# A second mixture of experts that sends each row to its two experts, in place of one that runs all eight

## The chip, the cores and the metric

One core of a Trainium2 chip runs the whole program. The metric is the device time of one execution in microseconds (us), median over runs. The engines are TensorE (PE, with its weight loads PEld), VectorE (DVE), ScalarE (ACT), GpSimd (POOL) and SyncE (SP), which issues DMAs.

## The reference

The program is two rounds of graph attention and mixture of experts over 6250 nodes of 256 features. Only its last step is touched:

```python
tokens = layernorm(x)                                   # 6250 x 256
probs = softmax(tokens @ router_w.T)                    # 8 experts
rw, re = top_k(probs, 2); rw = rw / max(rw.sum(-1), 1e-12)
out = tokens
for e in range(8):
    h = gelu(tokens @ w1[e] + b1[e])                    # 256 -> 256
    y = h @ w2[e] + b2[e]                               # 256 -> 256
    out = out + combine[:, e:e+1] * y                   # combine is 0 but for the two best
x = x + out
```

Everything is float32. The nodes are padded to 6400, which is 50 blocks of 128 rows.

## The kernel before

The program is a row of phases with a barrier (`end_phase`) between them. All node rows stay in one buffer in SBUF, `node`, of 51 blocks of 264 columns. Names in the trace carry the phase: `attn_` attention over edges, `gate_` the first mixture's router, `exp_` its experts, `pr_` projections for the second graph layer, `rel_` that layer, and `moe_` the second mixture, the last phase and the one that is replaced.

`feed_forward_top2` takes one block a turn. DVE divides the sums of the graph layer by their denominators (L2337 to L2340), adds the saved `x2` (L2342), takes the statistics (L587, L590), normalizes (L659) and adds the normalized row to `node` (L2325). PE transposes (L669), computes the router's logits (L2265), then for all eight experts the hidden features (`hidden`, L2227, four groups of four column tiles) and the outputs (`expert_pair`, L2238, two experts a call). ACT applies the GELU, 16 calls a block (L2211). DVE adds each expert's output times its weight to `node` (`mix_pair`, L2288), the weight being 0 for six of eight experts. POOL computes one power a block for the softmax (L2194) and one for the norm (L598). SP loads the weights once, loads `x2` and stores the result. The pipeline is written by hand, with semaphores, one in-order queue for each engine.

The first mixture already has the other scheme, with one expert a row. `attend_and_route` scatters each block of rows with an indirect DMA from POOL to the region of its expert in a table in HBM (L1186), fills up the rest of each region's last tile with 8 more scatters (L1205), and `expert_of_sorted` then takes 58 tiles of 128 sorted rows, each of one expert, whose number it reads from a table (L1449 hidden, L1528 output, L1553 bias, L1559 copy of the transposed tile). Its results are gathered back in the `pr_` phase (L1629).

## Time and profile before

| | us |
|---|---|
| median of 3 runs | 4670.19 (4669.13 to 4671.12) |
| the profiled execution | 4661.37 |
| its span in the profile | 4659.5 |
| last matmul of the second graph layer ends, second mixture begins | 3832 to 3834 |

| engine | busy us | share of the span |
|---|---|---|
| PE | 4005.9 | 86% |
| DVE | 3083.2 | 66% |
| POOL | 2281.4 | 49% |
| ACT | 2013.7 | 43% |

The shares are means over phases with different limits, so they say little of the last phase; the rows below are taken from it, and from earlier phases that already do what the change does. Times in the trace count from the start of the span.

### The profile page before, as it was taken

To read this page: it belongs to the slowest core of one execution; us is meant where nothing else is said; L and a number is where in the kernel's file an instruction comes from. 1 tells how busy PE (TensorE), PEld (TensorE's weight loads), DVE (VectorE), ACT (ScalarE), POOL (GpSimd) and SP (SyncE) were. 2 spreads that over 40 slices of the span, in tenths; PEclk is the share of its full clock that TensorE was granted. 3 is DMA by queue.
4 is the path that set the end of the run, shared out by engine and by line. 5 is a ranking of instruction groups with operands and counts; after the bars stand their busy time and mean duration, and the time that the engine had idled before them with its cause. 6 is when DMAs were issued, how large, how long until landed. Compare 5 with 4: busy or idle time off the path is not lost. (4 is left out here: it accounts for less than half of the span.)

```text
span 4659.5 us, 77523 instructions
## 1 busy us (share of the span) xinstructions
PE 4005.9 (86%) x21539; PEld 3198.9 (69%) x21540; DVE 3083.2 (66%) x8660; ACT 2013.7 (43%) x5648; POOL 2281.4 (49%) x2410
## 2 busy tenths in 40 slices
PE   8788888888888997999899777777777768999999
PEld 4566666666667996999544456655665647888888
DVE  5599999999995552111222278888888776666665
ACT  2455555555542332333233465656565532222222
POOL 5477777777762452000222277777777741111111
PEclk9999999999998998999899878788787789999999
DMA  6577777777763111111344555555555530000000
GB/s 214 184 205 203 207 204 205 206 204 202 205 172 136 40 39 49 37 36 35 117 183 174 196 173 158 170 165 161 168 160 167 155 116 30 16 16 17 17 16 12
DMA packets 233288, 602.19 MB, mean 129 GB/s; under 512 B 47156, under 2 KB 120024, under 8 KB 217128
## 3 DMA queue, kind: packets, MB, share of 16 engines
q0 software_dynamic: 119504, 368.96, 28.2%
q1 hardware_dynamic: 113496, 229.82, 14.0%
q8 instruction: 128, 2.10, 0.2%
q14 instruction: 160, 1.31, 0.1%
HBM read 494.26 MB, written 104.35 MB: 128 GB/s over the span
## 5 line engine op out<-in xcount | busy, mean ns | idle before, releaser
L274 POOL DMA_INDIRECT attn_KV<-kv_tab,attn_stage x880 | 930.9, 1058 | 280.1 <-issue 248.3
L1832 POOL DMA_INDIRECT rel_V<-h_tab,rel_stage x880 | 881.5, 1002 | 309.0 <-issue 238.8
L1935 PE MATMUL rel_SP<-rel_V,rel_OH 128*128 128x264 f32 x1760 | 608.3, 486 | 1.8 <-DVE node L2002 1.3
L387 PE MATMUL attn_SP<-attn_KV 128*128 128x264 f32 x1760 | 491.1, 404 | 25.5 <-DVE node L489 25.2
L375 PE MATMUL attn_QP<-node,attn_OHT 128*128 x1760 | 502.0, 410 | 10.8 <-issue 5.1
L2211 ACT ACTIVATE moe_HT<-moe_HB,moe_b 128x128 f32<-128x128 f32 x800 | 228.1, 368 | 565.4 <-PE moe_HB L2227 565.4
L1935 PEld LDWEIGHTS rel_SP<-rel_V,rel_OH 128*128 128x128 f32 x1760 | 382.1, 238 | 75.1 <-ACT rel_OH L1870 7.6
L387 PEld LDWEIGHTS attn_SP<-attn_KV 128*128 128x128 f32 x1760 | 341.5, 199 | 98.4 <-issue 42.2
L2227 PE MATMUL moe_HB<-moe_YT,moe_W 128*128 128x128 f32 x3200 | 401.8, 279 | 0.0
L2002 DVE TENSOR_TENSOR node<-node,rel_SP 128x264 f32 x880 | 366.3, 416 | 52.1 <-PE rel_SP L1935 31.5
L2227 PEld LDWEIGHTS moe_HB<-moe_YT,moe_W 128*128 128x128 f32 x3200 | 379.9, 193 | 19.3 <-issue 16.6
L2238 PE MATMUL moe_YE<-moe_W,moe_HT 128*128 128x256 f32 x1600 | 380.4, 381 | 0.0
L375 PEld LDWEIGHTS attn_QP<-node,attn_OHT 128*128 128x128 f32 x1760 | 330.0, 200 | 61.4 <-issue 16.2
L1728 PE MATMUL pr_H<-WX,pr_YT 128*128 128x512 f32 x800 | 353.8, 595 | 0.0
L450 DVE TENSOR_TENSOR attn_KV<-attn_KV,attn_QP 128x512 f32<-128x512 f32 x440 | 297.9, 677 | 58.2 <-DMA attn_KV<-kv_tab,attn_stage 57.6
L2238 PEld LDWEIGHTS moe_YE<-moe_W,moe_HT 128*128 128x128 f32 x1600 | 288.8, 190 | 33.8
L2008 DVE TENSOR_TENSOR rel_V<-rel_V 128x512 f32<-128x512 f32 x440 | 298.2, 678 | 0.0
L1923 PEld LDWEIGHTS rel_QP<-sd,rel_OHT 128*128 128x128 f32 x1760 | 274.6, 231 | 34.3 <-issue 19.9
L459 DVE TENSOR_REDUCE attn_ST<-attn_KV 128x16 f32<-128x512 f32 x440 | 297.7, 676 | 0.3
L467 DVE TENSOR_TENSOR attn_KV<-attn_KV 128x512 f32<-128x512 f32 x440 | 293.4, 677 | 0.0
L1923 PE MATMUL rel_QP<-sd,rel_OHT 128*128 x1760 | 276.0, 311 | 15.0 <-ACT rel_OHT L1853 15.0
L304 ACT ACTIVATE attn_far<-iota_f,dst_in 128x128 f32<-128x128 f32 x880 | 281.0, 391 | 3.6
(343 smaller groups left out, 6894.7 us busy)
## 6 DMA issues: line engine op xcount, KB each, us to landing
rel_OHT<-dst_rows SPq DMA_DIRECT2D x55, 1024.0 KB, 6.1
h_tab<-pr_H SPq DMA_DIRECT2D x50, 1056.0 KB, 4.0
attn_KV<-kv_tab,attn_stage POOLq DMA_INDIRECT x880, 3.7
rel_V<-h_tab,rel_stage POOLq DMA_INDIRECT x880
kv_tab<-qkv_KV SPq DMA_DIRECT2D x50, 256.0 KB, 2.1
attn_runs<-runs SPq DMA_DIRECT2D x55, 192.0 KB
rel_runs<-runs SPq DMA_DIRECT2D x55, 192.0 KB
Wd<-in_wd SPq DMA_DIRECT2D x8, 1024.0 KB
```

The costliest lines, as they stand in the source:

```text
L274: pool.indirect_dma_start(out=KV[:, i * IT + u, 0:2 * FEAT], out_offset=None, in_=d["kv_tab"][:, :], in_offset=bass.IndirectOffsetOnAxis(a ...
L375: mm = pe.matmul(QP[(2 * i + v) % BANKS][:, (u % 2) * FEAT:(u % 2 + 1) * FEAT], OHT[:, u, :], query(blks[v]), start=True, stop=True)
L387: mm = pe.matmul(SP[v % SUMS][:, 0:NUMC], KV[:, j * IT + u, 0:P], KV[:, j * IT + u, FEAT:ROW], start=(u % 2 == 0), stop=(u % 2 == 1))
L450: dve.tensor_tensor(keys, keys, QP[(2 * i + v) % BANKS][:, :].rearrange("p (s c) -> p s c", c=FEAT), ALU.mult).then_inc(s["product"], 1)
L1728: mm = pe.matmul(HP[g][:, :], f.YT[:, i, k * P:(k + 1) * P], WX[:, k, g * 512:(g + 1) * 512], start=(k == 0), stop=(k == 1))
L1832: pool.indirect_dma_start(out=V[:, i * IT + u, :], out_offset=None, in_=d["h_tab"][:, :], in_offset=bass.IndirectOffsetOnAxis(ap=stage[:, ...
L1923: mm = pe.matmul(QP[q // 2][:, (u % 8) * RH:(u % 8 + 1) * RH], OHT[:, k % 2, u, :], m.sd[:, bass.ds(blks[u // 2] * RH, RH)], start=True, s ...
L1935: pe.matmul(SP[(c * IT + u) % SUMS][:, 0:NUMC], OH[:, j * IT + u, :], V[:, j * IT + u, :], start=True, stop=True).then_inc(s["sums"], 1)
L2002: dve.tensor_tensor(acc, acc, SP[(c * IT + u) % SUMS][:, 0:NUMC], ALU.add).then_inc(s["added"], 1)
L2008: dve.tensor_tensor(rows, rows, V[:, at:at + 2, FEAT:NUMC].unsqueeze(3).to_broadcast([P, 2, HEADS, DH]), ALU.mult).then_inc(s["weighted"], 1)
L2227: mm = pe.matmul(HB[g % 2][:, (c % 4) * P:(c % 4 + 1) * P], W1[:, k, c * P:(c + 1) * P], f.YT[:, i, k * P:(k + 1) * P], start=(k == 0), st ...
L2238: mm = pe.matmul(YE[g][:, (e % 2) * FEAT:(e % 2 + 1) * FEAT], HT[:, 2 * e + k, :], W2[:, k, e * FEAT:(e + 1) * FEAT], start=(k == 0), stop ...
```

## The change

The last phase becomes three, with a barrier between each two.

`route_top2` normalizes the blocks, finds the two best experts of each row in chunks of five blocks (19 small DVE operations a chunk), gives each row a place in the regions of both experts, and scatters each block twice, 100 scatters from POOL. A scattered row is 260 columns: the normalized features and the number of the row's place in the result table. It adds the normalized row to `node` on ACT. It also loads the weights for the next phase, writes the spare tiles and, at its end, computes tables of each tile's expert and first row.

`experts_of_pairs` runs 107 tiles of 128 sorted rows: SP loads a tile from its base address, PE transposes it, DVE copies the tile's expert's first weights and bias (514 columns) into `own` and the transposed tile out of PSUM, PE computes the hidden features, ACT the GELU, PE the output with the second weights addressed by a register, DVE adds the bias into `R`, and POOL scatters `R` to the rows named in column 256 of the tile, into `y_out`, where the two results of a node lie side by side. Rings are 4 deep for the loaded tiles and the results.

`mix_top2` loads 256 KB of `y_out` a block on SP, adds the two rows times their weights on DVE and stores 128 KB from ACT's queue.

```diff
--- before.py
+++ after.py
+TOP = 2
+CHUNK = 5
+SORTED2 = (TOP * NPAD + EXPERTS * (P - 1)) // P
+ROW2 = FEAT + 4
...
-def feed_forward_top2(nc, m, d):
...
+def route_top2(nc, m, d):
...
+    RING, XR, OUTS2 = 25, 4, 5
+    NORM, COUNT, ROUTE = 6, 7, 11
+    ROUTED, SCATTER = 19, 16
...
+                def load(b):
+                    need(sp, s["x3"], b - XR + 1)
+                    sp.dma_start(X[:, b % XR, :], d["x2"][b * P:(b + 1) * P, :]).then_inc(x_in[b % XR], 16)
+                for b in range(XR):
+                    load(b)
...
+                for b in range(XR, 2 * XR):
+                    load(b)
+                sp.wait_ge(s["zeroed"], 3)
+                for k in range(EXPERTS):
+                    sp.dma_start(d["y2"][SPARE + k * P:SPARE + (k + 1) * P, :], Z[:, EXPERTS + k, :]).then_inc(s["spare"], 16)
+                sp.dma_start(m.V1[:, :], d["m1"][:, :]).then_inc(s["spare"], 16)
+                for b in range(2 * XR, 3 * XR):
+                    load(b)
+                for k in range(2):
+                    sp.dma_start(m.V2[:, k, :], d["m2"][k * P:(k + 1) * P, :]).then_inc(s["spare"], 16)
+                sp.dma_start(m.c2[:, :], d["mb2"][0:1, :].to_broadcast([P, EXPERTS * FEAT])).then_inc(s["spare"], 16)
+                for b in range(3 * XR, BLOCKS):
+                    load(b)
+                sp.wait_ge(s["spare"], 16 * (EXPERTS + 4))
...
+                def scale(c):
+                    n, i = size(c), c % 2
+                    pool.wait_ge(s["mv"], c * CHUNK + n)
...
+                def scatter(b):
+                    u = b // OUTS2
+                    pool.wait_ge(s["slotted"], b // CHUNK + 1)
+                    pool.wait_ge(s["rows"], 3 * (b + 1))
...
+                    need(pool, out[b % OUTS2], u * 16 * TOP)
+                    for k in range(TOP):
+                        pool.indirect_dma_start(out=d["y2"][:, :],
+                                                out_offset=bass.IndirectOffsetOnAxis(ap=slot[:, k, b:b + 1], axis=0),
+                                                in_=Y2[:, b % RING, k, :], in_offset=None).then_inc(out[b % OUTS2], 16)
...
+                pool.memset(Z[:, :, :], 0.0).then_inc(s["zeroed"], 1)
...
+                for t in turns:
+                    if t % CHUNK == 0 and has(t // CHUNK - 1, CHUNKS2):
+                        scale(t // CHUNK - 1)
+                    if has(t - SCATTER, BLOCKS):
+                        scatter(t - SCATTER)
...
+                for e in range(EXPERTS):
+                    pool.indirect_dma_start(out=d["y2"][:, :],
+                                            out_offset=bass.IndirectOffsetOnAxis(ap=beyond[:, e:e + 1], axis=0),
+                                            in_=Z[:, e, :], in_offset=None).then_inc(s["pad"], 16)
...
+                for b in range(BLOCKS):
+                    c, i = b // CHUNK, b % CHUNK
+                    row, j = b % RING, c % 2
+                    act.wait_ge(s["shift"], 2 * (c + 1))
+                    if b >= RING:
+                        act.wait_ge(out[(b - RING) % OUTS2], ((b - RING) // OUTS2 + 1) * 16 * TOP)
+                    act.activation(Y2[:, row, 0, 0:FEAT], node(b), ACT.Identity, bias=shift[:, j, i:i + 1],
+                                   scale=rstd[:, j, i:i + 1]).then_inc(s["rows"], 1)
...
+                    act.activation(node(b), node(b), ACT.Identity, bias=shift[:, j, i:i + 1],
+                                   scale=plus[:, j, i:i + 1]).then_inc(s["based"], 1)
...
+                def route(c, k):
...
+                    if k == 11:
+                        step(dve.tensor_tensor(of(both), of(hot[0]), of(hot[1]), ALU.add))
+                    if k == 12:
+                        dve.wait_ge(s["counted"], c + 1)
+                        step(dve.tensor_tensor(of(place), cnt, filled[:, :].unsqueeze(1).to_broadcast([P, n, EXPERTS]), ALU.add))
...
+                    if k == 18:
+                        step(dve.tensor_copy(slot[:, :, c * CHUNK:c * CHUNK + n], spot[:, :, w]))
+                        dve.wait_ge(s["choice"], at + 1)
+                        dve.sem_inc(s["slotted"], 1)
...
+                for t in turns:
+                    c, i = t // CHUNK, t % CHUNK
+                    q = t - ROUTE
+                    chunk, part = q // CHUNK, q % CHUNK
                     if has(t, BLOCKS):
+                        dve.tensor_tensor(heads(node(t)), heads(node(t)), inv[:, t, :].unsqueeze(2).to_broadcast([P, HEADS, DH]),
+                                          ALU.mult).then_inc(s["scaled"], 1)
+                    route(chunk, 4 * part)
+                    if has(t, BLOCKS):
+                        dve.wait_ge(s["scaled"], t + 1)
+                        dve.wait_ge(x_in[t % XR], (t // XR + 1) * 16)
+                        dve.tensor_tensor(node(t), node(t), X[:, t % XR, :], ALU.add).then_inc(s["x3"], 1)
+                    route(chunk, 4 * part + 1)
+                    if has(t, BLOCKS):
+                        dve.wait_ge(s["x3"], t + 1)
+                        dve.bn_stats(st[:, :], node(t)).then_inc(s["stats"], 1)
+                    route(chunk, 4 * part + 2)
+                    if t % CHUNK == NORM % CHUNK and has(t // CHUNK - 1, CHUNKS2):
...
+                    if has(t, BLOCKS):
+                        dve.wait_ge(s["stats"], t + 1)
...
+                        dve.bn_aggr(mv[:, c % 2, i, :], st[:, :]).then_inc(s["mv"], 1)
+                    route(chunk, 4 * part + 3)
+                tables()
...
+def experts_of_pairs(nc, m, d):
...
+    BATCH, YR, RR = 12, 4, 4
+    KB = FEAT // P
+    WROW = KB * FEAT + KB
...
+                    need(sp, s["turned"], t - YR + 1)
+                    need(sp, s["dest"], t - YR + 1)
+                    sp.dma_start(Y[:, t % YR, :], d["y2"][bass.ds(base[t % BATCH], P), :]).then_inc(y_in[t % YR], 16)
+            @block.gpsimd
+            def _(pool):
+                for t in range(SORTED2):
+                    pool.wait_ge(s["dest"], t + 1)
+                    pool.wait_ge(s["out"], t + 1)
+                    pool.indirect_dma_start(out=d["y_out"][:, :],
+                                            out_offset=bass.IndirectOffsetOnAxis(ap=dest[:, t % RR:t % RR + 1], axis=0),
+                                            in_=R[:, t % RR, :], in_offset=None).then_inc(sent[t % RR], 16)
...
+                for t in range(SORTED2):
+                    act.wait_ge(s["hidden"], t + 1)
+                    need(act, s["made"], t - 1)
+                    for c in range(KB):
+                        act.activation(HT[:, t % 2, c * P:(c + 1) * P], HB[t % 2][:, c * P:(c + 1) * P], ACT.Gelu,
+                                       bias=own[:, t % 2, KB * FEAT + c:KB * FEAT + c + 1]).then_inc(s["gelu"], 1)
+            @block.tensor
+            def _(pe):
+                def turn(t):
+                    if has(t, SORTED2):
+                        pe.wait_ge(y_in[t % YR], (t // YR + 1) * 16)
+                        need(pe, s["yT"], t - 1)
+                        for k in range(KB):
+                            mm = pe.transpose(T[t % 2][:, k * P:(k + 1) * P], Y[:, t % YR, k * P:(k + 1) * P], m.ident[:, :])
+                        mm.then_inc(s["turned"], 1)
...
+                for t in range(SORTED2 + 1):
+                    if has(t, SORTED2):
+                        pe.wait_ge(s["yT"], t + 1)
+                        pe.wait_ge(s["own"], t + 1)
+                        need(pe, s["gelu"], KB * (t - 1))
+                        for c in range(KB):
+                            for k in range(KB):
+                                at = k * FEAT + c * P
+                                mm = pe.matmul(HB[t % 2][:, c * P:(c + 1) * P], own[:, t % 2, at:at + P],
+                                               YT[:, t % 2, k * P:(k + 1) * P], start=(k == 0), stop=(k == KB - 1))
+                        mm.then_inc(s["hidden"], 1)
+                    turn(t + 2)
                     n = t - 1
+                    if has(n, SORTED2):
+                        if n % BATCH == 0:
+                            e = experts_of(n, mybir.EngineType.PE)
+                        pe.wait_ge(s["gelu"], KB * (n + 1))
+                        need(pe, s["out"], n - 1)
+                        for k in range(KB):
+                            mm = pe.matmul(RB[n % 2][:, 0:FEAT], HT[:, n % 2, k * P:(k + 1) * P],
+                                           m.V2[:, k, bass.ds(e[n % BATCH] * FEAT, FEAT)], start=(k == 0), stop=(k == KB - 1))
+                        mm.then_inc(s["made"], 1)
...
+                def own_weights(t):
+                    if has(t, SORTED2):
+                        if t % BATCH == 0:
+                            experts.append(experts_of(t, mybir.EngineType.DVE))
+                        need(dve, s["hidden"], t - 1)
+                        need(dve, s["gelu"], KB * (t - 1))
+                        dve.tensor_copy(own[:, t % 2, :], m.V1[:, bass.ds(experts[t // BATCH][t % BATCH] * WROW, WROW)]
+                                        ).then_inc(s["own"], 1)
+                def copy_turned(t):
+                    if has(t, SORTED2):
+                        dve.wait_ge(y_in[t % YR], (t // YR + 1) * 16)
+                        if t >= RR:
+                            dve.wait_ge(sent[t % RR], t // RR * 16)
+                        dve.tensor_copy(dest[:, t % RR:t % RR + 1], Y[:, t % YR, FEAT:FEAT + 1]).then_inc(s["dest"], 1)
+                        dve.wait_ge(s["turned"], t + 1)
+                        need(dve, s["hidden"], t - 1)
+                        dve.tensor_copy(YT[:, t % 2, :], T[t % 2][:, 0:FEAT]).then_inc(s["yT"], 1)
...
+                for t in range(1, SORTED2 + 1):
+                    own_weights(t + 1)
+                    copy_turned(t + 1)
+                    n = t - 1
+                    dve.wait_ge(s["made"], n + 1)
+                    if n >= RR:
+                        dve.wait_ge(sent[n % RR], n // RR * 16)
+                    e = experts[n // BATCH][n % BATCH]
+                    dve.tensor_tensor(R[:, n % RR, :], RB[n % 2][:, 0:FEAT], m.c2[:, bass.ds(e * FEAT, FEAT)], ALU.add
+                                      ).then_inc(s["out"], 1)
...
+def mix_top2(nc, m, d):
...
+        rows = d["y_out"].rearrange("(n k) c -> n (k c)", k=TOP)
+        with nc.Block() as block:
+            @block.sync
+            def _(sp):
+                for b in range(BLOCKS):
+                    need(sp, s["mixed"], TOP * (b - YR + 1))
+                    sp.dma_start(Y[:, b % YR, :], rows[b * P:(b + 1) * P, :]).then_inc(y_in[b % YR], 16)
+            @block.scalar
+            def _(act):
+                for b in range(BLOCKS):
+                    act.wait_ge(s["mixed"], TOP * (b + 1))
+                    act.dma_start(d["out"][b * P:(b + 1) * P, :], node(b)).then_inc(s["stored"], 16)
...
+            @block.vector
+            def _(dve):
+                for b in range(BLOCKS):
+                    dve.wait_ge(y_in[b % YR], (b // YR + 1) * 16)
+                    for k in range(TOP):
+                        need(dve, s["mixed"], TOP * b + k)
+                        dve.scalar_tensor_tensor(node(b), Y[:, b % YR, k * FEAT:(k + 1) * FEAT], m.mix[:, k, b:b + 1], node(b),
+                                                 ALU.mult, ALU.add).then_inc(s["mixed"], 1)
...
+            route_top2(nc, m, d)
+            end_phase(nc, m)
+            experts_of_pairs(nc, m, d)
+            end_phase(nc, m)
+            mix_top2(nc, m, d)
...
+    "y2": ((SPARE + EXPERTS * P, ROW2), F32),
+    "y_out": ((TOP * NPAD + 2 * EXPERTS * P, FEAT), F32),
```

## Rows read from the trace of the kernel before

**Rows 1.** Windows: busy us (and instructions) by engine, granted clock, DMA share, GB/s
```profile
300.00:400.00 100.00, 83.95 (x404) 63.60 (x402) 96.02 (x221) 57.42 (x154) 77.76 (x74) 0.97 0.71 203
1800.00:2240.00 440.00, 423.65 (x2900) 396.25 (x2900) 44.71 (x122) 132.26 (x464) 0.00 (x0) 0.98 0.12 37
3000.00:3100.00 100.00, 76.20 (x353) 59.85 (x353) 80.27 (x214) 58.56 (x157) 76.85 (x77) 0.79 0.53 155
...
3837.00:3850.00 13.00, 0.69 (x2) 0.29 (x2) 3.28 (x11) 0.00 (x0) 0.76 (x2) 0.50 0.83 338
3850.00:4640.00 790.00, 777.43 (x5153) 698.45 (x5154) 513.57 (x1770) 224.77 (x785) 118.41 (x148) 0.99 0.05 16
```

**Rows 2.** Chain that ended last, in the last phase: start, us, what
```profile
4595.44 0.22 PE moe_T L669 x2
4595.66 1.79 PE moe_HB L2227 x16
...
4597.55 1.73 PE moe_YE L2238 x8
...
4611.09 0.22 PE moe_T L669 x2
...
4656.36 0.50 DVE node L2288
```

**Rows 3.** Groups by form: shapes, count, busy us, mean ns, idle before
```profile
L2079 DVE MEMSET node<- 128x13464 f32 x1 | 11.3, 11278 | 2.8 <-issue 2.8
L678 ACT COPY pr_YT<-pr_T 128x256 f32<-128x256 f32 x50 | 18.9, 378 | 36.3 <-PE pr_T L669 36.3
```

**Rows 4.** Timeline of DVE at the last phase's start: sum, statistics, their combination
```profile
3852.79 0.42 DVE L2342 TENSOR_TENSOR node<-node,moe_X 128x256 f32<-128x256 f32 x1
3853.14 0.42 DVE L587 BATCH_NORM_STATS2 moe_st<-node 128x6 f32<-128x256 f32 x1
3853.70 0.18 DVE L590 BATCH_NORM_AGGREGATE moe_mv<-moe_st 128x2 f32<-128x6 f32 x1
```

**Rows 5.** Groups on POOL in the first mixture's router phase
```profile
L1186 POOL DMA_INDIRECT y_sorted<-gate_Y,slot x50 | 51.6, 1032 | 11.2 <-issue 9.3 <-DMA y_sorted<-gate_Y,slot 2.0
L598 POOL TENSOR_TENSOR gate_rstd<-gate_rstd,mhalf 128x1 f32<-128x1 f32 x50 | 28.0, 560 | 4.2
```

**Rows 6.** Timeline of POOL, end of the first mixture's router phase
```profile
1782.56 0.96 POOL L1186 DMA_INDIRECT y_sorted<-gate_Y,slot  x1 [0.95 <-DMA y_sorted<-gate_Y,slot]
...
1796.36 0.96 POOL L1205 DMA_INDIRECT y_sorted<-gate_zeros,gate_beyond  x1 [0.30 <-issue]
```

**Rows 7.** Timeline of SP's queue: first load of the phase after it
```profile
1805.74 0.36 SPq L1489 DMA_DIRECT2D exp_Y<-y_sorted  x1
```

**Rows 8.** Groups by form on DVE: a copy inside SBUF, two that read PSUM
```profile
L867 DVE CAST prep_rawf_dst<-prep_raw_dst 128x896 f32<-128x896 int32 x1 | 0.6, 617 | 0.0
L1553 DVE TENSOR_TENSOR exp_R<-exp_RB,exp_bd 128x256 f32<-128x256 f32 x58 | 24.6, 425 | 373.4 <-PE exp_RB L1528 373.4
L1559 DVE COPY exp_YT<-exp_T 128x256 f32<-128x256 f32 x58 | 24.1, 415 | 25.5 <-PE exp_T L1537 25.5
```

**Rows 9.** The scatters' line, L1186: issue to landing of its 50 scatters
```profile
DMA to landing us min/median/max: 2.4/2.5/3.7
```

**Rows 10.** Timeline, start of the projection phase: an index copy and its gather
```profile
2246.79 0.15 DVE L1687 COPY pr_row_of<-row_in 128x1 int32<-128x1 int32 x1
...
2247.77 1.19 POOL L1629 DMA_INDIRECT pr_R<-r_tab,pr_row_of  x1 [4.56 <-DVE pr_row_of L1687]
```

**Rows 11.** DMA issues, last phase: count, KB each, median us to landing
```profile
moe_X<-x SPq DMA_DIRECT2D x50, 128.0 KB, 2.0
```

**Rows 12.** DMA queues of the page: packets, MB, share of 16 engines
```profile
q0 software_dynamic: 119504, 368.96, 28.2%
q1 hardware_dynamic: 113496, 229.82, 14.0%
```

**Rows 13.** Line L274, attention's gathers: ns min/median/max
```profile
L274 POOL DMA_INDIRECT attn_KV<-kv_tab,attn_stage x880: 942/946/1898, 178.7 to 1376.1; - x176
```

More of the change, by code:

```diff
@@ L2199, in _ @@
+                for b in range(BLOCKS - OUTS2, BLOCKS):
+                    pool.wait_ge(out[b % OUTS2], (b // OUTS2 + 1) * 16 * TOP)
+                pool.wait_ge(s["pad"], 16 * EXPERTS)
             @block.scalar
             def _(act):
[L2201 to L2212 removed]
@@ new lines, in _ @@
+                pe.wait_ge(s["weights"], 32)
+                pe.wait_ge(s["ones"], 2)
+                for b in range(BLOCKS + COUNT + CHUNK):
+                    if has(b, BLOCKS):
+                        pe.wait_ge(s["rows"], 3 * b + 1)
+                        need(pe, s["yT"], b - 1)
+                        for k in range(2):
+                            mm = pe.transpose(T[b % 2][:, k * P:(k + 1) * P], Y2[:, b % RING, 0, k * P:(k + 1) * P], m.ident[:, :])
+                        mm.then_inc(s["turned"], 1)
+                    if b % CHUNK and b < BLOCKS:
+                        logits(b - 1)
+                    if b % CHUNK == CHUNK - 1 or b == BLOCKS - 1:
+                        logits(b)
+                    if b % CHUNK == COUNT % CHUNK:
+                        count((b - COUNT) // CHUNK)
```

473 lines of the change are left out of this document (284 added, 189 removed).

## The prediction

> **What bounds the kernel now.** I read the page first (PE is busy 86% of the span), then the windows by stage, then the chain in the last phase, because only that phase changes. In the windows [rows 1] the reader is to see that from 3850 to 4640 us PE is busy 777 of 790 us at a granted clock of 0.99 (its 2.4 GHz level), and the DMA engines 5%. The chain [rows 2] shows why: nearly nothing but PE, and block after block the same order. From one transpose to the next, 4595.44 to 4611.09, is 15.65 us. Four groups of hidden features at 1.79 and four of outputs at 1.73 are 14.1 of it. So the phase is a matmul stream in which six of eight experts are multiplied by 0. It starts at 3833.5 and ends with the span at 4659.5: 826 us, of which 50 x 15.65 = 783 are the stream.
>
> **What is taken away and what comes.** The whole phase of 826 us goes. In its place stand three phases in series; I cost each by what ends last in it.
>
> **Phase A, routing.** DVE waits for POOL's memset of 16 x 260 = 4160 columns: a memset of 13464 took 11.28 us [rows 3], so 3.5, and with what lies around it about 5 us to the first turn. A turn of DVE without routing is four operations: the rows give sum to statistics 0.35, statistics to combination 0.56, combination 0.18 [rows 4], and one more of the first size with its hand-over, 0.5: 1.6 us. From turn 11 on four small operations lie between them, at some 0.2 each; they partly fill waits of the others, so 1.9 (bounds 1.6 and 2.4). POOL's first scatter stands at turn 16 and needs the fifth routing step of chunk 0, so it comes after 5 + 11 x 1.6 + 5 x 1.9 = 32 us. SP issues 3.1 MB of second weights and biases ahead of the load of block 12, and a load behind weights waits for them: 338 GB/s in the stretch of the weights before [rows 1] makes 9 us from about turn 8, of which some 4 are not covered. First scatter at 36 us.
>
> From there POOL ends last. It issues 100 scatters: mean 1.03 us each beside a working DVE [rows 5], and 0.30 between two [rows 6], together 1.26 (0.96 + 0.30) to 1.33; I take 1.30, 130 us. Queued between them on POOL are the norm's two small operations for 7 more chunks, 0.56 for the power [rows 5] and about as much again, 8 us. DVE's 39 later turns at 1.9 to 2.4 are 74 to 94 us, and ACT's four passes of 256 columns at 0.38 [rows 3] are below 2 us a block against POOL's 2.8, so both are ahead and the ring of 25 blocks does not fill. Then 8 scatters for the tiles' rests, 1.27 each [rows 6]: 10. The hand-over to the next phase has one example with scatters last: the last one ends at 1797.32 [rows 6], the next phase's first load is issued at 1805.74 [rows 7], 8.4 us. Phase A: 36 + 130 + 8 + 10 + 8 = 192 us.
>
> **Phase B, 107 tiles.** PE: four hidden matmuls are half of 1.79 (16 rows are 8 calls), two output matmuls half of 1.73, two transposes 0.22 [rows 2]: 0.90 + 0.87 + 0.22 = 1.98 us a tile. DVE: the copy of 514 columns, by 617 ns for 896 [rows 8], is between 0.35 in proportion and 0.62, say 0.44; the row numbers 0.15 [rows 10], the transposed tile 0.42 and the bias 0.43 [rows 8]: 1.4 us. POOL: one scatter, 1.3. So by work alone PE is the bound, 1.98.
>
> But DVE's queue holds a wait that PE's stream has not: `copy_turned(t)` waits until the scatter of tile t-4 has landed, and behind it in the same queue stand the copy for PE and the bias of tile t-2, whose scatter the copy of tile t+2 waits for. This loop is two tiles long: copy of the row numbers 0.15, transposed tile 0.42, bias 0.43, POOL's start after a wait 0.83 (the index copy ended at 2246.94, the gather began at 2247.77 [rows 10]), issue to landing 2.5 [rows 9]: 4.3 us, 2.16 a tile. A longer loop through PE spans three tiles: bias 0.43, 0.83, 2.5, 0.15, 0.42, then hidden, transpose and output 1.98, and some 0.3 for hand-overs: 6.6, 2.2 a tile. I take 2.2 a tile, 235 us. Bounds: 1.98 if the landing is hidden, 2.8 with the longest landing of the row, 3.7. Filling the pipeline (load 2.0 [rows 11], transpose, copies, first matmuls at 1.2 GHz) is 7 us, reading the tables of experts into registers 0 to 5, say 2, the last tile's output, bias and scatter 3.5, and the hand-over with scatters last 8.4. Phase B: 7 + 235 + 2 + 4 + 8 = 256 us.
>
> **Phase C, the mixing.** A block moves 384 KB. The hardware queues moved 229.82 MB in 14.0% of the engines' span of 4659.5 us, 352 GB/s while busy [rows 12]: 1.12 us. DVE has two operations of 0.50 in a chain [rows 2]: 1.04. I take 1.2 (bounds 1.04 and 1.9, the latter if loads and stores hinder each other as much as their times together), 60 us, with 2 us for the first load [rows 11] and 2 for the last store: 64 us.
>
> **The sum.** 192 + 256 + 64 = 512 us in place of 826: 314 less, a span of 4346 and a profiled execution of 4661.4 - 314 = 4347. The median of the runs shown is 8.8 us above the profiled execution; the same distance gives 4356, so I say 4357.
>
> **A rule against the change.** Phase B puts a copy of 514 float32 columns from SBUF to SBUF on DVE beside POOL's scatters in every tile. The row that bears on it takes 617 ns for 896 columns, hardly more than the 415 of the 256 columns that come out of PSUM [rows 8], so copies inside SBUF go at a pace of their own; no row has one beside a scatter. The Trainium skill (page SBUF — State Buffer, section SBUF: two separate sides) states that such a copy (float32, SBUF to SBUF) runs in a mode that uses two ports and locks GpSimd out of the shared ports, so that it cannot write the descriptors of its DMA. By the rows alone the tile takes 2.2 us; by the rule each scatter would be held for up to the copy, 0.44, which the two-tile loop turns into 2.4 a tile, and that is part of the second rival.
>
> **The rivals.**
> (1) No loop binds: phase B at PE's 1.98, POOL at 1.26 a scatter, phase C at 1.1. That is 24 + 4 + 5 = 33 less, 4324. For it: the ring is 4 deep and the landing row is 2.5 at a light load. Against: the two-tile loop needs less than 4.0 and its rows add to 4.3. Chance 0.17.
> (2) DVE's copy and POOL's descriptor writing hold each other up. A scatter would grow by 0.44, or at most to the longest gather in the trace, 1.9 [rows 13]; the two-tile loop then takes 4.7 to 5.2, which is 2.4 to 2.6 a tile: 21 to 43 more, about 4390. For it: the gathers' spread of 942 to 1898 ns [rows 13] shows that something holds POOL at times. Against: their median is 946. Chance 0.14.
> (3) PE's clock falls. At 76% PE busy the granted clock was 0.79, at 84% it was 0.97, at 96% 0.98 [rows 1]. Phase B has PE at 1.98 of 2.2, 90%. If the loops leave more holes, 0.79 would make PE's tile 1.98 / 0.79 = 2.5: 32 more, 4389; at 1.2 GHz all through it is 3.96, 188 more, 4545. Chance 0.1, and 0.03 of it for the end above 4450.
> (4) The DMAs are slower than at light load: landing 3.7 in phase B (0.6 a tile, 64) and 1.9 a block in phase C (35), up to 4455. Chance 0.08.
> (5) The other side, slower than before: each indirect DMA costs POOL much more. With d more on each, phase A grows by 108 d; phase B runs at the larger of (4.3 + d) / 2 and 1.3 + d a tile. At d = 1.9 that is 205 + 107 x 1.0 = 312 more, and the gain is gone: the point is a scatter of 2.9 us in place of 1.0. The longest of 880 gathers is 1.9 [rows 13]. Chance 0.03.
> The forecast itself has 0.48, with a range of its own from 4335 to 4380.
>
> **How the numbers follow.** The time is the forecast's. The range takes in (1), (2), the lighter part of (3) and most of (4): 4308 to 4450; about 0.1 lies outside. Within 0.2%, 9 us, is about what a measurement of this kernel can't tell from no change; to land there all of 305 us must be lost, 0.01. Faster 0.96, slower 0.03.
>
> **What the next profile would show.** Right: about 192 us from the first scaling of a block to the first load of a sorted tile, with POOL the busiest engine, scatters 1.3 us apart from about 36 us on; then 107 tiles 2.2 us apart, with DVE's copy of the row numbers waiting for a DMA and PE's clock above 0.9; then 50 blocks 1.2 us apart. Wrong, if scatters in the tiles' phase are much longer than 1.0 us (the second rival), if PE waits for nothing and the clock is low (the third), if loads of `y_out` land late in the last phase (the fourth). What would upset the sum most is POOL: it is nearly alone on the path of phase A, and any cost on its queue that these rows don't show is paid a hundred times.

## The result, and the profile after

The changed kernel takes 4436.98 us (median of 4 runs, 4432.29 to 4439.15), the kernel before 4670.65 beside it: a ratio of 0.9497, 95% interval 0.9481 to 0.9514. Forecast were 4357 with a range of 4308 to 4450. The direction and the range held; the time is 80 us above the forecast, near the slow end, and where these 80 us lie is the subject of what follows.

The change made three phases, A (routing), B (the tiles' experts) and C (mixing). In the windows of the changed kernel (columns as in [rows 1]) they end at about 4092, 4377 and 4437:

```profile
3886.00:4050.00 164.00, 128.93 (x577) 118.48 (x577) 61.59 (x317) 77.88 (x200) 97.03 (x101) 0.50 0.29 95
4050.00:4092.00 42.00, 5.34 (x26) 5.24 (x25) 9.07 (x30) 0.50 (x2) 21.23 (x22) 0.50 0.20 73
4092.00:4377.00 285.00, 233.16 (x1498) 197.30 (x1498) 135.94 (x436) 68.48 (x217) 103.21 (x107) 0.97 0.34 100
4377.00:4437.00 60.00, 0.00 (x0) 0.00 (x0) 48.43 (x100) 0.00 (x0) 0.00 (x0) 0.50 0.93 328
```

Four lines of the tiles' views give the edges (ns min/median/max, first and last start): the scatters of phase A, the loads of sorted tiles, the scatters of results, and the loads of phase C.

```profile
L2230 POOL DMA_INDIRECT y<-route_Y,route_slot x100: 957/962/1167, 3886.4 to 4068.8; - x100
...
L2511 SPq DMA_DIRECT2D pair_Y<-y x107: 332/333/362, 4092.6 to 4351.4; - x107
...
L2518 POOL DMA_INDIRECT y_out<-pair_R,pair_dest x107: 955/957/1172, 4101.9 to 4364.8; - x107
...
L2634 SPq DMA_DIRECT2D mix_Y<-y_out x50: 319/320/433, 4377.1 to 4426.3; - x50
```

Phase A runs from VectorE's first operation at 3839.14 to the first load of a sorted tile at 4092.64: 253.5 us, forecast 192. Phase B lasts to 4377.06: 284.4, forecast 256. Phase C: 60.3, forecast 64. With earlier phases 5.6 us longer than in the profiled execution before, that is 61.5 + 28.4 - 3.7 + 5.6 = 92 us above the 4347 forecast for the profiled execution; it took 4439.15. The median is only 80 above its forecast, by luck: it was put 10 us above the profiled execution and came 2 below.

**Phase A.** The scatters are as forecast, 0.96 us and 0.30 between. But 100 of them take 182.4 us, not 130. The waits of the phase (us in total, times, longest) say who is late:

```profile
DVE route_place L2370 <- PE route_CNT L2306: 111.4, 10, 13.3
POOL route_rstd L2217 <- DVE route_mv L2462: 75.4, 10, 17.7
```

and the timeline of one chunk of five blocks shows the order of it:

```profile
3973.10 1.00 PE L2304 MATMUL route_CNT<-route_both,route_before 128*128 128x8 f32 x4
...
3981.89 0.20 DVE L2370 TENSOR_TENSOR route_place<-route_CNT,route_filled 128x40 f32<-128x40 f32 x1 [11.50 <-PE route_CNT L2306]
3982.92 0.18 DVE L2462 BATCH_NORM_AGGREGATE route_mv<-route_st 128x2 f32<-128x6 f32 x1
...
3983.19 0.41 POOL L2217 TENSOR_SCALAR route_rstd<-route_mv 128x5 f32<-128x5 f32 x1 [5.05 <-DVE route_mv L2462]
...
3985.26 1.06 POOL L2230 DMA_INDIRECT y<-route_Y,route_slot  x1 [0.20 <-issue]
```

The reader is to see one in-order chain. TensorE counts how many rows of the chunk go to each expert (`count`): 20 float32 products of 8 columns, which the records show as 40, from 3973.10 to 3981.78, 0.217 us each at a granted clock of 0.50, the 1.2 GHz level. VectorE stands at step 12 of the routing (L2370) until they are done, 11.5 us (2.7 of them before the count starts, while TensorE has transposes and logits ahead of it in its queue), and the next blocks' scaling and statistics stand behind it in its queue. GpSimd reaches the norm of the next chunk and waits for these statistics, 5.05 us, with scatters that have all they need queued behind. A chunk takes 19.77 us (L2370 from 3962.12 to 3981.89), and without that wait GpSimd has 14.7.

**Phase B.** 106 tile periods take 4364.8 - 4101.9 = 262.9 us, 2.48 each, forecast 2.2. Filling and leaving (9.3 and 12.3) are as forecast, PE's clock is 0.97. In the timeline of VectorE and GpSimd:

```profile
4200.13 0.15 DVE L2588 CAST pair_dest<-pair_Y 128x1 int32<-128x1 f32 x1 [1.59 <-DMA y_out<-pair_R,pair_dest]
...
4200.57 0.41 DVE L2605 TENSOR_TENSOR pair_R<-pair_RB,c 128x256 f32<-128x256 f32 x1
...
4201.74 0.96 POOL L2518 DMA_INDIRECT y_out<-pair_R,pair_dest  x1 [1.83 <-DVE pair_dest L2588]
...
4204.44 0.15 DVE L2588 CAST pair_dest<-pair_Y 128x1 int32<-128x1 f32 x1 [0.58 <-DMA y_out<-pair_R,pair_dest]
...
4205.02 1.16 PE L2555 MATMUL pair_HB<-pair_YT,pair_own 128*128 128x128 f32 x8
...
4206.23 1.03 PE L2566 MATMUL pair_RB<-V,pair_HT 128*128 x4
...
4207.39 0.15 DVE L2588 CAST pair_dest<-pair_Y 128x1 int32<-128x1 f32 x1 [1.51 <-DMA y_out<-pair_R,pair_dest]
...
4207.83 0.41 DVE L2605 TENSOR_TENSOR pair_R<-pair_RB,c 128x256 f32<-128x256 f32 x1
```

Both loops of the prediction are in it. The two-tile loop goes from the row numbers at 4200.13 over the scatter at 4201.74 to the row numbers at 4204.44: 4.31 us, forecast 4.3. The three-tile loop goes from the bias at 4200.57 over the same scatter, hidden features and outputs to 4207.26, where TensorE is done: 6.69, forecast 6.6. But the bias can't start there: VectorE stands at the row numbers of another tile until 4207.39, for that tile's scatter. It starts at 4207.83, so the loop takes 7.26, 2.42 a tile. This is one stretch of the timeline; the mean of all tiles is 2.48.

**Phase C.** VectorE adds the two rows of a block one after the other. It waits for a load once, at the start, and then takes 1.11 us a block without a wait, so it sets the pace here and not the DMAs:

```profile
4427.53 7.66 DVE L2649 SCALAR_TENSOR_TENSOR node<-mix_Y,mix,node 128x256 f32<-128x256 f32 x14
```

### The profile page after: what moved, and what is told of

It is laid out like the page before. It is cut to its first block and busy times, and to the rows that moved or that the text cites. A ratio compares the mean times of both kernels' runs of the same rounds, so it can differ in the third digit from the quotient of the medians.

```text
span 4437.4 us, 68970 instructions
## 1 busy us (share of the span) xinstructions
PE 3607.2 (81%) x18487; PEld 2833.4 (64%) x18488; DVE 2838.7 (64%) x7838; ACT 1951.7 (44%) x5314; POOL 2396.5 (54%) x2499
## 5 line engine op out<-in xcount | busy, mean ns | idle before, releaser
L1633 POOL DMA_INDIRECT pr_R<-r_tab,pr_row_of x50 | 50.2, 1003 | 467.8 <-DVE pr_row_of L1691 448.7
L1865 ACT ACTIVATE rel_far<-iota_f,dst_in 128x128 f32<-128x128 f32 x880 | 278.5, 388 | 0.0
L1515 ACT ACTIVATE exp_HT<-exp_HB,b 128x128 f32<-128x128 f32 x464 | 132.6, 368 | 323.2 <-PE exp_HB L1453 323.2
L1557 DVE TENSOR_TENSOR exp_R<-exp_RB,exp_bd 128x256 f32<-128x256 f32 x58 | 24.6, 424 | 373.4 <-PE exp_RB L1532 373.4
L1732 PEld LDWEIGHTS pr_H<-WX,pr_YT 128*128 128x128 f32 x800 | 149.1, 191 | 168.8 <-issue 168.5
## 6 DMA issues: line engine op xcount, KB each, us to landing
kv_tab<-qkv_KV SPq DMA_DIRECT2D x50, 256.0 KB, 2.2
mix_Y<-y_out SPq DMA_DIRECT2D x50, 256.0 KB, 4.3
```

The lines of the kernel that those rows point to most:

```text
L1732: mm = pe.matmul(HP[g][:, :], f.YT[:, i, k * P:(k + 1) * P], WX[:, k, g * 512:(g + 1) * 512], start=(k == 0), stop=(k == 1))
```

## Experiments

The runs fall into sets (the recorded expectations say "call"); each set ran on one chip, with the kernel before beside it. Phases by the same edges as above, in us; time and ratio to the kernel before of the same set. Sets 2 and 3 ran on chips on which the kernel before itself takes 5030 and 5057 us; the earlier phases are longer there. In sets 0, 1 and 4 it takes 4670 to 4671, so their times are compared as they stand; with the other sets only phases, and differences to the kernel before, are compared.

| set | kernel | time | ratio (95%) | below before | phase A | phase B |
|---|---|---|---|---|---|---|
| 0 | changed kernel | 4436.98 | 0.9497 (0.9481, 0.9514) | 233.7 | 253.5 | 284.4 |
| 1 | count in bfloat16 | 4388.42 | 0.9396 (0.9381, 0.9412) | 281.5 | 202.0 | 277.3 |
| 1 | count twice | 4524.04 | 0.9690 (0.9674, 0.9706) | 145.9 | 338.7 | 282.6 |
| 1 | rings of 8 | 4394.66 | 0.9407 (0.9392, 0.9423) | 275.2 | 253.2 | 234.4 |
| 1 | copy on ScalarE | 4436.63 | 0.9502 (0.9486, 0.9518) | 233.3 | 253.6 | 279.9 |
| 2 | count by wide matmuls | 4770.08 | 0.9482 (0.9458, 0.9507) | 259.5 | 216.8 | 283.5 |
| 2 | weights later | 4792.26 | 0.9530 (0.9505, 0.9555) | 237.4 | 254.4 | 279.5 |
| 2 | only results' ring 8 | 4761.23 | 0.9472 (0.9440, 0.9503) | 268.4 | 256.0 | 234.8 |
| 2 | all three | 4710.32 | 0.9369 (0.9350, 0.9387) | 319.3 | 210.8 | 233.7 |
| 3 | changed kernel again | 4824.66 | 0.9547 (0.9528, 0.9566) | 232.5 | 255.7 | 276.9 |
| 3 | all, weights spread | 4736.71 | 0.9372 (0.9352, 0.9393) | 320.4 | 211.7 | 234.6 |
| 3 | TensorE kept busy | 4835.82 | 0.9560 (0.9540, 0.9579) | 221.3 | 266.2 | 282.3 |
| 4 | bfloat16 and rings | 4341.77 | 0.9303 (0.9291, 0.9316) | 328.5 | 202.1 | 234.5 |

Phase B with the ring of results at 4 spreads from 277 to 284, so 7 us there is nothing.

**1. The count in bfloat16.** In `route_top2`:

```diff
-        before = sb("before", [P, P], F32)
-        ones = sb("ones", [P, P], F32)
+        before = sb("before", [P, P], BF16)
+        ones = sb("ones", [P, P], BF16)
...
-        both = sb("both", [P, CHUNK, EXPERTS], F32)
+        both = sb("both", [P, CHUNK, EXPERTS], BF16)
```

> In phase A only: the three operands of the counting matmuls (the strict triangle, the ones, the sum of the two choices) are bfloat16 instead of float32; they hold 0 and 1 alone, so every count stays exact. Theory A (the counting on TensorE is what sets the chunk period of 19.8 us: VectorE stands 11.5 us a chunk at step 12, the next blocks' scaling and statistics stand behind it, and GpSimd then waits 5.05 us a chunk for them): the count's 40 records of 0.217 us become 20 shorter ones, at most 4.3 us instead of 8.7, and the period falls by 4.3 to 5.05 us, to about 15, where GpSimd's own work of 14.7 us a chunk stands; the kernel falls by 43 to 50 us, to 4387 to 4394. Rival A2 (GpSimd's own instructions set the period, and VectorE's wait is only slack): no change, 4437. Rival A3 (the scale step or ACT sets it): VectorE's wait shrinks, the period doesn't, change under 10 us.

48.6 us less, phase A 51.5 less. The first line of its timeline to the next operation of VectorE is the whole count of one chunk:

```profile
3985.83 0.19 PE L2304 MATMUL route_CNT<-route_both,route_before 128*128 128x8 bf16 x2
...
3986.12 0.38 PE L2306 MATMUL route_CNT<-route_both,route_ones 128*128 128x8 bf16 x9
...
3986.61 0.20 DVE L2370 TENSOR_TENSOR route_place<-route_CNT,route_filled 128x40 f32<-128x40 f32 x1 [3.56 <-PE route_CNT L2306]
```

0.67 us for 20 records where float32 took 8.7 for 40: far less than the 4.3 that I had allowed. VectorE still waits 3.56 us, 2.8 of them for TensorE's work ahead of the count, but GpSimd has no gap above 0.4 us from its first scatter to its last scatter of filling rows; it is the bound, as the prediction had it, and its 100 scatters take 139.0 us (forecast 138 with the norms). Rivals A2 and A3 are out.

**2. The count twice.**

```diff
+                        for again in range(2):
                             for i in range(n + 1):
```

> In phase A only: the whole group of counting matmuls is issued twice, with the same result. Theory A: another 8.7 us a chunk on the loop, ten chunks, 87 us more, about 4524. Rivals A2 and A3: the 11.5 us in which VectorE stands are partly slack, so less than 40 us more, and nothing if VectorE's wait is all slack.

87.1 us more, where ten chunks at 8.7 give 87. So a longer count is paid in full.

**3. Rings of 8.** In `experts_of_pairs`:

```diff
-    BATCH, YR, RR = 12, 4, 4
+    BATCH, YR, RR = 12, 8, 8
```

> In phase B only: the ring of loaded rows, the ring of results and the ring of destinations hold 8 tiles instead of 4, with a semaphore for each. Theory B (the tile period of 2.48 us is set by the loop through the ring of results: VectorE reads a tile's destinations only when the scatter of the tile four before has landed, and 73.6 us of its waits end with a landing): the landing goes off the loop, and the period falls to between VectorE's and TensorE's own 2.0 and 2.2 us, so 30 to 51 us less, 4386 to 4407. Rival B2 (VectorE's weight copy and GpSimd's descriptor writing hold each other up, the rule of the Trainium skill, page 'SBUF — State Buffer', section 'SBUF: two separate sides'): the rings don't matter, the period stays at 2.4 to 2.5, change under 10 us. Rival B3 (TensorE sets the period): the wait moves from the landing to TensorE's results, change under 10 us.

42.3 us less. TensorE now never waits long, and the tile takes 1.98 us (4202.20 to 4204.18; 2.00 in the mean), the sum of TensorE's work in the prediction:

```profile
4202.20 0.42 DVE L2605 TENSOR_TENSOR pair_R<-pair_RB,c 128x256 f32<-128x256 f32 x1 [0.82 <-PE pair_RB L2566]
4202.55 0.42 DVE L2580 COPY pair_own<-V 128x514 f32 x1
...
4203.39 0.96 POOL L2518 DMA_INDIRECT y_out<-pair_R,pair_dest  x1 [1.02 <-DVE pair_dest L2588]
...
4204.18 0.42 DVE L2605 TENSOR_TENSOR pair_R<-pair_RB,c 128x256 f32<-128x256 f32 x1 [0.82 <-PE pair_RB L2566]
```

B2 and B3 are out: had another cost set the period, the rings would not have moved it by a fifth.

**4. The weight copy on ScalarE,** behind the two Gelus of tile t; its calls on VectorE go.

```diff
+                    act.wait_ge(s["gelu"], KB * (t + 1))
+                    own_weights(t + 2)
...
-                        dve.tensor_copy(own[:, t % 2, :], m.V1[:, bass.ds(experts[t // BATCH][t % BATCH] * WROW, WROW)]
-                                        ).then_inc(s["own"], 1)
+                        act.copy(own[:, t % 2, :], m.V1[:, bass.ds(experts[t // BATCH][t % BATCH] * WROW, WROW)]
+                                 ).then_inc(s["own"], 1)
```

> In phase B only: the copy of a tile's own weights and bias (128x514) is made by ScalarE behind its two Gelu instructions, not by VectorE; rings stay at 4. Theory B (the landing of the scatter): the copy stands before the late wait, not in the loop, so the landing stays the last to come and the period moves by less than 0.1 us, under 10 us in all. Rival B2 (VectorE's copy blocks GpSimd's descriptor writing): the scatters start sooner after the result, their instructions shorten below 955 ns, and the period falls by 0.2 to 0.4 us, 21 to 43 us in all. Rival B4 (VectorE's own work is the bound): the period falls by up to the copy's 0.42 us, 45 us in all, and VectorE's waits grow by as much less. If ScalarE's copy comes too late for TensorE, the period grows instead.

No change (4436.63 to 4436.98), as theory B said:

```profile
L2518 POOL DMA_INDIRECT y_out<-pair_R,pair_dest x107: 956/958/962, 4114.2 to 4372.3; - x107
...
  DMA y_out<-pair_R,pair_dest: 117.9, 100
```

The second line is what ended VectorE's idle time: the landings, 117.9 us against 80.5 in the changed kernel. VectorE has less to do and stands longer at the same wait.

The first line, beside 955/957/1172 in the changed kernel, bears on the second rival: its longest scatters are gone. In most tiles VectorE's copy ends before the scatter starts, which comes 0.76 us after the end of the bias operation. In 9 of the changed kernel's 107 tiles the two overlap. In five of these the copy began 0.09 to 0.21 us before the scatter, and the scatter took 1.05 to 1.17 us; in the other four it kept 0.96. One of each kind:

```profile
4213.43 0.43 DVE L2580 COPY pair_own<-V 128x514 f32 x1 [0.67 <-PE pair_HB L2555]
4213.52 1.17 POOL L2518 DMA_INDIRECT y_out<-pair_R,pair_dest  x1 [1.02 <-DVE pair_R L2605]
...
4306.98 0.96 POOL L2518 DMA_INDIRECT y_out<-pair_R,pair_dest  x1 [1.34 <-DVE pair_R L2605]
4307.11 0.43 DVE L2580 COPY pair_own<-V 128x514 f32 x1 [0.89 <-ACT pair_HT L2532]
```

All five end 0.82 to 0.83 us after the copy does. With the copy on ScalarE the two overlap in 94 tiles, and no scatter takes more than 0.962. The rule of the Trainium skill (page SBUF — State Buffer, section SBUF: two separate sides), that such a copy on VectorE locks GpSimd out, agrees with these scatters. The five are 0.8 us longer in all, which is why moving the copy changes nothing.

**5. The count by 6 wide float32 matmuls.**

```diff
-        both = sb("both", [P, CHUNK, EXPERTS], F32)
+        both = sb("both", [P, CHUNK + 1, EXPERTS], F32)
...
+                        seen = both[:, :, :].rearrange("p b e -> p (b e)")
+                        mm = pe.matmul(CNT[:, 0:(n + 1) * EXPERTS], before[:, :], seen[:, 0:(n + 1) * EXPERTS], start=True, stop=False)
+                        for k in range(1, n + 1):
+                            mm = pe.matmul(CNT[:, k * EXPERTS:(n + 1) * EXPERTS], ones[:, :], seen[:, 0:(n + 1 - k) * EXPERTS],
+                                           start=False, stop=(k == n))
```

> In phase A only: the counts of a chunk are made by 6 float32 matmuls of 48 down to 8 columns instead of 20 of 8 columns, with the same sums (the sum of the two choices has a sixth block of zeros behind it, so that one product with the triangle opens all 48 columns; then each product with the ones adds block k's choices to all blocks behind it). Theory A, the number of records is the cost: 12 records of 0.22 to 0.3 us are 2.6 to 3.6 us instead of 8.7, the period falls by GpSimd's whole wait of 5.05 us, to the same 15 as with bfloat16, so 4385 to 4394. Rival A4 (bfloat16 itself brought the gain, by a rate, not by fewer records; with float32 kept the wide matmuls of 48 columns take as much longer as they are fewer): less than half of that gain, over 4412.

Its phase A is 39.2 us shorter than the 256.0 of the same set with this phase unchanged (run 7), eight tenths of the 51.5 of run 1. One count takes 2.7 us (4300.20 to 4302.91) for 12 records, 0.23 us each with 48 to 8 columns, against 0.217 with 8. So in float32 the record is the price, not its columns, as theory A said. The rest of the gain did not come, because in nine of the ten chunks VectorE's wait ends 1.1 to 3.8 us after TensorE's last record, where it is 0.11 in runs 1 and 2 (more on this at the end). In the whole time the gain is smaller: 259.5 us below the kernel before, where the changed kernel is 232.5 to 233.7 below, so 26 to 27 of the 48.6 us, just above the half at which rival A4 was set. The shape of the count, not the time, tells the two apart.

**6. Weights later.** In SyncE's queue the 12 transfers (zero rows, `V1`, `V2`, `c2`) stand behind all loads of `x2`, not among them:

```diff
+                for b in range(2 * XR, BLOCKS):
+                    load(b)
                 sp.wait_ge(s["zeroed"], 3)
...
-                for b in range(2 * XR, 3 * XR):
-                    load(b)
...
-                for b in range(3 * XR, BLOCKS):
-                    load(b)
```

> In phase A only: SyncE issues the eight stores of zero rows, the first weights (2.1 MB), the second weights and the biases behind all loads of x2, not between the loads of blocks 7 and 12. Theory D (the first scatter comes at 48 us of the phase and not at 36 because VectorE stands 6.64 and 2.90 us for block 8's and block 12's rows, which queue behind the weights in the DMA queues): the first scatter comes 9 us sooner, and all of it is kept, since GpSimd's later scatters follow it at a fixed period: 4426 to 4430. Rival D2 (the first scatters wait for the counting of the chunks anyway): under 3 us. Rival D3: the late weights are not there when phase B begins, which takes back 5 to 10 us: 4432 to 4440.

Theory D fell. Its phase A is 254.4, 1.6 below the 256.0 of the same set, and the first scatter comes 45.8 us after the start, 47.6 there. VectorE's waits for block 8's and block 12's rows are gone, but in exchange it waits for the first logits and longer at the first step 12:

```profile
4224.58 0.20 DVE L2343 TENSOR_REDUCE route_most<-route_LG 128x5 f32<-128x40 f32 x1 [5.12 <-PE route_LG L2291]
...
4241.05 0.20 DVE L2368 TENSOR_TENSOR route_place<-route_CNT,route_filled 128x40 f32<-128x40 f32 x1 [11.56 <-PE route_CNT L2304]
```

The 5.12 is new, and 11.56 stands in place of the 8.58 of the changed kernel. The time held is D2's, under 3 us; of its reason, the count, only a part is seen, the larger part is the logits.

**7. Only the ring of results at 8.**

```diff
-    BATCH, YR, RR = 12, 4, 4
+    BATCH, YR, RR = 12, 4, 8
```

> In phase B only: the rings of results and destinations hold 8 tiles, the ring of loaded rows stays at 4. Theory B (the scatter's landing is late at the ring of results): the same as with both rings at 8, about 4394. Rival B5 (the ring of loaded rows was the one that bound: the load of a tile is issued only when the tile four before has been turned and its destinations read): nearly nothing, 4430 to 4437, or part of the gain if both bind.

Phase B is 234.8 against 234.4 with both rings. It is the results' and destinations' ring alone.

**8 and 9. Everything together, with the weights behind the loads, and then among them.**

> All three: counting by 6 bfloat16 matmuls, rings of 8 in phase B, weights behind the loads of x2. Each sits in another phase or another wait, so the gains add: 48.6 us of the counting, 42.3 of the rings, 5 to 9 of the weights; 4336 to 4342. If the weights' gain is the same wait as the counting's (both stand ahead of the first scatter), 4346. A phase A of about 195 us and a phase B of about 234 us.

> The changed kernel as it is, beside the other two of this call on the same chip: 0.9497 of the kernel before, as measured at first, and a phase A of 254 us and a phase B of 277 to 285 us, whichever theory holds.

```diff
+                    if b == 18:
+                        sp.wait_ge(s["zeroed"], 3)
+                        for k in range(EXPERTS):
+                            sp.dma_start(d["y2"][SPARE + k * P:SPARE + (k + 1) * P, :], Z[:, EXPERTS + k, :]).then_inc(s["spare"], 16)
+                    if b in (22, 34):
...
+                    if b == 26:
+                        sp.dma_start(m.V1[:, :], d["m1"][:, :]).then_inc(s["spare"], 16)
+                    if b == 30:
+                        sp.dma_start(m.c2[:, :], d["mb2"][0:1, :].to_broadcast([P, EXPERTS * FEAT])).then_inc(s["spare"], 16)
```

> Counting by 6 bfloat16 matmuls and rings of 8, with the zero rows, the weights and the biases issued one at a time behind the loads of blocks 18, 22, 26, 30 and 34. Theory D4 (weights ahead of block 8 hold up the start by some 2 us; weights behind the last load fill the DMA queues while the last blocks' scatters should land, which took 8.4 us of GpSimd's time; in the middle GpSimd has 15 blocks of work before it and hides them): phase A falls from 210.7 to about 200, the kernel is 95 to 100 us below the changed kernel of the same call. Rival: the transfers in the middle hold up the scatters' landing just as well, phase A stays at about 210, 85 to 90 us below.

The changed kernel behaves on these chips as on the first (232.5 us below the kernel before; 233.7 there), though its ratio is 0.9547 where 0.9497 was expected, since the same gain is taken from a longer time. Against it the two versions gain 86.8 and 87.9, some 10 less than each expectation. Both end with the same hole, and spreading the weights did not close it: my reading of the eighth run, that late weights fill the DMA queues, fell with the ninth. What the trace of the ninth shows instead (ScalarE and GpSimd near the end of phase A):

```profile
4377.15 0.37 ACT L2264 COPY route_YT<-route_T 128x256 f32<-128x256 f32 x1 [2.47 <-remote]
...
4387.04 0.37 ACT L2264 COPY route_YT<-route_T 128x256 f32<-128x256 f32 x1 [9.51 <-remote]
...
4399.91 0.96 POOL L2232 DMA_INDIRECT y<-route_Y,route_slot  x1 [8.71 <-DVEq L2385]
```

TensorE's transposes for these two copies are recorded by 4374.66, and ScalarE's waits for them end 2.5 us and 12.4 us later. From there the last chunk's places are late and GpSimd stands 8.71 us.

**10. TensorE kept busy,** in the loop over blocks:

```diff
+                    if b < BLOCKS:
+                        for again in range(4):
+                            pe.matmul(idle_out[:, :], m.ident_b[:, :], idle_in[:, :], start=True, stop=True)
```

> In phase A only: for each block TensorE is given four more bfloat16 matmuls of 512 columns behind the logits, into a bank that nobody reads. Theory E (the granted clock of 0.50 in phase A, 1.2 GHz, doubles the price of the counting, and it would rise if TensorE were given long matmuls between): the granted clock of the phase rises towards 1.0, the 40 records of a count take 4.4 us instead of 8.7, and the phase falls by 20 to 50 us. Rival E2 (the clock stays at 0.50): the added matmuls, 4 of 0.4 us a block, lie in front of the count on TensorE's queue, and the phase grows by 10 to 40 us.

Phase A grew by 10.5 us against the same set. The granted clock rose to only 0.64 over the phase:

```profile
4284.00:4460.00 176.00, 156.76 (x733) 118.53 (x739) 61.50 (x316) 79.00 (x201) 95.80 (x100) 0.64 0.27 88
```

The mean hides two levels. In the second count (windows on `route_CNT` and PE alone: busy, records, granted clock, DMA) the first records ran at 1.00 and the last ones at 0.50, and the timeline gives six records in 0.67 us at the upper level:

```profile
4293.90:4296.20 2.30, 2.30 (x22) 1.00 0.20 65
4296.60:4299.90 3.30, 3.30 (x16) 0.50 0.00 0
...
4295.19 0.81 PE L2308 MATMUL route_CNT<-route_both,route_ones 128*128 128x8 f32 x6
4295.86 0.37 PE L2306 MATMUL route_CNT<-route_both,route_before 128*128 128x8 f32 x2
```

A record is 0.112 us at the 2.4 GHz level and 0.214 at 1.2. The ten counts took 6.2 to 9.2 us, 7.9 in the mean against 8.7. So the first half of theory E holds, the low clock doubles the price: at the upper level throughout, a count would take 40 x 0.112 = 4.5 us (an estimate from these records), and ten of them would take 42 us less. The forecast gain did not come: two counts ran at 0.50 throughout, the others at 1.00 for a part only, and GpSimd's wait grew from 5.07 to between 6.4 and 8.6 us a chunk. That the added matmuls, which stand ahead of the count in TensorE's queue, make it grow is argued, not shown. The phase went E2's way, with a clock that was not E2's.

**11. The two small edits together**, runs 1 and 3 in one kernel.

> The two small edits together and nothing else: the counting's operands in bfloat16 (still 20 matmuls), and rings of 8 in phase B; the weights stay where the changed kernel loads them. If the gains are independent they add: where the kernel before takes 4670 us, 48.6 and 42.3 below 4437 are 4346, a ratio of 0.9306; phase A 202 us, phase B 234 us. On a chip like those of the last two calls (kernel before at 5030 to 5057) phase A tells two theories apart. Theory F (there a wait on TensorE's semaphore ends 1 to 3 us late whenever GpSimd scatters without a pause, whatever the form of the counting): about 211 us, as with the 6 wide matmuls. Rival F2 (the lag comes from the wide matmuls): 202 us.

4341.77 us, 0.9303: the gains add (0.9306 forecast), and this is the fastest version relative to the kernel before. It ran where the kernel before takes 4670 us, so it does not tell F from F2.

## Why the prediction was right in direction and 80 us off

**Which step failed.** "DVE's 39 later turns at 1.9 to 2.4 are 74 to 94 us, and ACT's four passes ... are below 2 us a block against POOL's 2.8, so both are ahead." One operation was left out of it: `count`, 20 matmuls a chunk in the middle of the routing steps, was not costed, neither as work of TensorE nor as a wait in VectorE's in-order queue. With the wait a chunk takes 19.77 us, not the 14 of GpSimd. Runs 1 and 2 show cause and size: made cheap it gives 48.6 us back, doubled it costs 87.1. Nor was it asked at which clock TensorE would run there; it was granted 0.50, which by the records of run 10 is about half of the price. In the same sentence ScalarE's passes were too cheap: those of 256 columns take 0.36 to 0.60 us, with the small copy 2.3 us a block, which is still below 2.8.

**Phase A's other terms.** With the count cheap the first scatter comes at 38.9 us (forecast 36), the scatters take 139.0 (138), and the phase 202 (192). That 139.0 meets 138 is partly luck: most scatters are 1.27 apart, not 1.30, and seven norms cost 11.8 us, not 8. The rest is the end, where the hand-over from the last scatter of filling rows took 12.9 instead of 8.4. In the changed kernel itself the first scatter came at 47.3: the first count is in it, too. The wait for weights, priced at 9 us of which 4 uncovered, was 9.5, with 6.64 of it at block 8, behind the first weights and zero rows that were not in the sum; but nearly all of it was covered by the waits for the logits and the count (run 6: 1.8 us at the first scatter).

**Phase B.** The mechanism was right, the size of a term was off: "I take 2.2 a tile", measured 2.48 in the profile. Each loop had its length, 4.31 and 6.69; two loops that share an in-order queue delay each other, and I took the longer one's mean instead. Runs 3 and 7 show that the landing behind the ring of results sets it; 4 shows that VectorE's copy doesn't. That it is the two loops' meeting which makes 2.2 into 2.48 is read from the timeline; no run separates it.

**The rivals.** The first (nothing binds, 1.98 a tile) is what the rings of 8 give; its 1.26 a scatter and 1.1 a block were nearly what the changed kernel has. The second's size (2.4 to 2.6 a tile) came by another cause: its own mechanism lengthens 5 of 107 scatters, 0.8 us in all (run 4), because in most tiles the copy ends before the scatter starts. The third did not occur in phase B, 0.97; in phase A, where it was not looked for, the clock stayed at 0.50. The fourth did not: landing 2.4/2.6/4.7 against 2.4/2.5/3.7 in [rows 9]. The fifth did not: 0.96 a scatter. Phase C at 60.3 had 1.11 a block, not 1.2. That is near the bare DMA figure of 1.12 by chance: VectorE's chain, priced at 1.04, sets it, and loads land ahead of it.

## What to carry to other kernels

Before summing an engine's durations, list every instruction on which another engine waits inside the loop, tiny ones too, and ask what stands behind that wait in the queue: 200 products of 8 columns held this kernel up by 49 us. Where two loops pass through one in-order queue, the longer one's length is only a lower bound of the period: add what one makes the other wait, or deepen the ring until a landing is out of both. A count of zeros and ones is exact in bfloat16, so the type costs nothing there.

## What the runs showed of the hardware

- A float32 product of 8 columns costs 0.43 us (two records) at the 1.2 GHz level and 0.22 at 2.4 (run 10), and one of 48 hardly more; in bfloat16 it is one record, and 20 take 0.67 us at the 1.2 GHz level, thirteen times less than in float32. The weight loads differ too: 104 ns in bfloat16, 333 in float32. The Trainium skill (page TensorE: Matmul & The Clock Gate, section Weight-path perf modes — Fast Weight Load (FWL) and DoubleRow) says that the fast load needs 128 weights and a type other than float32; the two durations agree with it.
- A 128x514 float32 copy inside SBUF on VectorE lengthened a scatter from 0.96 to as much as 1.17 us when it had begun 0.09 to 0.21 us before it (run 4). When it began later, or ran on ScalarE, the scatter kept its length.
- In phase A the records have TensorE busy 128.9 of 164 us at a granted clock of 0.50, in phase B 233 of 285 at 0.97.
- Chips differ: the kernel before takes 4670 us on some and 5030 to 5057 on others. In the versions of the changed kernel phase A starts at 3837 to 3855 us on the former and at 4199 to 4238 on the latter, while the same phases agree within 8 us. Why is not shown.
- On the chips of sets 2 and 3, while GpSimd scatters without a pause, VectorE's wait for the count often ends 1 to 4.8 us after TensorE's last record; elsewhere it is 0.11. The changed kernel has it there too, at its last two chunks (1.15 and 2.32 us), so the wide matmuls are not its only cause. Run 10, on the same chip, has 0.11 in all ten. And no kernel with 20 short matmuls and a GpSimd without pauses ran on such a chip, so theory F is neither shown nor excluded, and the cause of the hole of 8.7 us stays open.
